# Keys, queries and values of a tile as one fp32 product in a two-layer GNN kernel

## Chip, core and metric

The kernel runs on one core of a Trainium2 chip. The metric is the device time of one execution in microseconds (us). Engines are named as in the profile: PE is TensorE (PEld its weight loads), ACT is ScalarE, DVE is VectorE, POOL is GpSimd, SP is the engine that issues most transfers. Everything discussed here happens in the first of two stages, in which node features and the tables for the second stage are made.

## What is computed

There are 6250 nodes of 128 features, 200000 edges sorted by destination, 4 node types and 8 edge types. The first layer averages the neighbours of each node, applies a linear layer and normalises. The second layer is an attention over edges; its queries, keys and values are products with a matrix that depends on the type of the node.

```python
def _type_matmul(h, W, types):
    out = jnp.zeros_like(h)
    for t in range(W.shape[0]):
        out = out + jnp.where((types == t)[:, None], h @ W[t], 0.0)
    return out

x = _layernorm(x + relu(concat([x, neigh_mean]) @ W.T + b))      # first layer
Q, K, V = (_type_matmul(x, W, node_type) for W in (W_Q, W_K, W_V))
k_t = _type_matmul(K[src], W_edge, edge_type)                    # per edge
scores = jnp.sum(Q[dst] * k_t, axis=-1) / scale * mu[edge_type]
out = segment_sum(V[src] * sparse_softmax(scores, dst)[:, None], dst)
x = _layernorm(x + out)
```

## The kernel before

**Two stages.** The nodes are cut into 49 tiles of 128. The first stage (up to about 1360 us of the profiled span) sums the neighbours, computes the first layer for each tile and writes, for each node, 8 rows (one for each edge type) of key times edge matrix beside the value, to the table `kv_table` in HBM, and the queries to `queries_t`. The second stage (the rest of the span) gathers table rows for each edge and does the attention. The change touches the first stage only.

**The sweep.** `sweep(l0)` goes through 50 steps `i`. On PE, step `i` is a loop over `h` = 0 to 48. Each `h` is one bf16 matmul of 385 columns (`slot_sum`, L715) for the neighbour sums; at every third `h` comes a `pick` (L708, 392 columns), whose result ACT copies (`take`, L1007) before the pick after next may be written to the same PSUM bank. Groups of 8 matmuls (`run_sum`, L738) stand at `h` = 0 and 22, and `node_sum` (L727) at `h` = 3 waits for DVE's `join_parts` (L1280). All engines work strictly in the order in which their instructions are written.

**What a tile needs inside the sweep.** In step `i` the tile `i - 2` ("early") gets its first layer: PE transposes (L745 at `h` = 30, L750 at 35) and the product L755 to L757 at 40, then DVE's `relu` (L1336) and `normalise_x1`, which leaves `x1_typed`: the tile's rows, one copy for each of the 4 types, zeroed where the node has another type. The tile `i - 3` ("late") gets its projections: at `h` = 8 PE transposes the four copies (L763) and ACT copies them to SBUF (L1024, after take 3). At `h` = 13 `project_keys` (L771) multiplies with `wk_s` as the stationary operand, so that the keys come out transposed, at `h` = 16 `project_values` (L776) with the rows as stationary operand, so that values come out as rows, and at `h` = 19 `project_queries` (L780), again transposed. Each is four fp32 matmuls of 128 columns added up in PSUM. ACT copies the transposed keys to `kT` after take 5 (`copy_key`, L1028) and, after take 7, the values 8 times over into `kv_rows` (L1034, which also waits until the previous tile's table rows are stored) and the queries to `q_tile` (L1037). Then PE multiplies the keys with the edge matrices, `low_keys` (L786, `h` = 25) and `high_keys` (L789, `h` = 28), 512 columns each; DVE copies the low half (L1357) and ACT the high half (L1041), and SP stores.

**Order.** Nothing schedules this by itself: the numbers `h ==` on PE and `c ==` on ACT are the order. 47 tiles have their late part inside the sweep (steps 3 to 49). Step 49 has no picks. The last two tiles have it behind the sweep in `late_part`, where the same functions follow one another with nothing between them.

**PSUM.** Keys go to bank 7, shared with `node_sum` and `high_keys`; values and queries to bank 5, shared with the first layer's transposes and product.

## Time and profile before

| | us |
|---|---|
| median of 3 runs | 3727.59 (3725.5 to 3731.58) |
| the profiled execution, whole | 3697.22 |
| its span, first to last instruction | 3695.4 |

The rows quoted below come from that one profiled execution. PE, ACT, DVE, POOL busy over the whole span: 2551.0, 1124.1, 1530.9 and 2372.2 us. An fp32 matmul shows as two records ("x8" for four matmuls); an fp32 transpose is one record. A record of PE is drawn longer than the time that it holds the engine, because matmuls are pipelined: the next one starts while the record before is still open. What a matmul costs is therefore read from start to start.

### The profile page before, as it was taken

The numbers are of one execution on the slowest core, as the hardware profiler recorded it, in microseconds if no ns is written. First come the engines' busy times: TensorE is split into PE (matmuls) and PEld (weight loads), VectorE is DVE, ScalarE is ACT, GpSimd is POOL, SyncE is SP. The second block draws the span as 40 slices with busy tenths as digits, with TensorE's granted clock in tenths as the row PEclk, the third lists the DMA queues.
The fourth block names the chain that finished last, engine by engine and source line by source line (L and its number), as shares of the span: only waits on it lengthen the run. The fifth ranks groups of instructions, "written<-read, shape, count | busy, mean of one in ns | idle before, by whom it ended". The sixth has DMA issues, their size and how long they took to land.

```text
span 3695.4 us, 38864 instructions
## 1 busy us (share of the span) xinstructions
PE 2551.0 (69%) x13692; PEld 1754.7 (47%) x13692; DVE 1530.9 (41%) x4283; ACT 1124.1 (30%) x2072; POOL 2372.2 (64%) x2400
## 2 busy tenths in 40 slices
PE   1688888888888861666666666666676666666667
PEld 0355555555555541444444444444444444444445
DVE  8466666666666620222222222222222222222223
ACT  3333444444444420222222222222222222222222
POOL 6656667676666617566666666666666666666662
PEclk9799999999999985777777777777777777777778
DMA  4233344443444313233333333333333333333331
GB/s 135 64 98 115 107 130 120 119 120 107 120 120 120 112 68 107 72 96 96 97 97 96 97 97 96 97 97 96 97 97 97 97 97 96 96 97 97 97 97 43
DMA packets 195810, 369.81 MB, mean 100 GB/s; under 512 B 62177, under 2 KB 126509, under 8 KB 189347
## 3 DMA queue, kind: packets, MB, share of 16 engines
q0 software_dynamic: 112432, 281.92, 27.5%
q1 hardware_dynamic: 76679, 82.09, 6.7%
q10 hardware_dynamic: 6508, 3.33, 0.3%
q8 instruction: 111, 1.82, 0.2%
q14 instruction: 80, 0.66, 0.1%
HBM read 299.89 MB, written 67.30 MB: 99 GB/s over the span
## 4 chain that ended last, share of the span: by engine, by line
PE 38%; another core or an unknown queue 20%; issue 19%; ACT 14%; DVE 8%; ACTq 1%; DMA 0%; DVEq 0%; POOLq 0%; POOL 0%; SPq 0%
PE banks L715 8%; ACT work L1090 5%; PE banks L872 4%; PE banks L886 4%; PE banks L901 3%; PE banks L708 3%; ACT work L1098 3%; ACT picks L1007 2%; PE banks L738 2%; DVE sums L1269 2%; PE banks L771 1%; PE banks L908 1%; PE banks L866 1%; PE banks L776 1%
## 5 line engine op out<-in xcount | busy, mean ns | idle before, releaser
L655 POOL DMA_INDIRECT ring<-kv_table,src_n x1264 | 1207.9, 956 | 625.9 <-issue 368.8
L650 POOL DMA_INDIRECT ring<-x_part_rows,work x512 | 538.0, 1051 | 249.2 <-issue 138.4
L886 PE MATMUL banks<-identf,ring 128*128 128x128 f32 x1264 | 242.9, 319 | 646.5 <-ACT work L1098 458.2
L1007 ACT ACTIVATE picks<-banks 128x392 bf16<-128x392 f32 x800 | 396.6, 499 | 730.0 <-PE banks L708 646.7
L715 PE MATMUL banks<-sums,picks 128*128 128x385 bf16 x2450 | 617.6, 335 | 0.4 <-ACT picks L1007 0.4
L886 PEld LDWEIGHTS banks<-identf,ring 128*128 128x128 f32 x1264 | 169.4, 162 | 698.9 <-ACT work L1098 506.4
L1090 ACT ACTIVATE work<-banks,negmax 128x2048 f32<-128x2048 f32 x98 | 193.0, 1969 | 905.9 <-issue 668.4
L1098 ACT ACTIVATE work<-banks 128x512 f32<-128x512 f32 x392 | 213.0, 598 | 816.1 <-remote 689.1
L1467 DVE SCALAR_TENSOR_TENSOR sums<-sums,corr,banks 128x128 f32<-128x128 f32 x98 | 34.0, 347 | 936.5 <-remote 928.9
L1448 DVE TENSOR_REDUCE largest<-banks 128x1 f32<-128x2048 f32 x98 | 224.6, 2292 | 468.9 <-PE banks L872 252.3
L872 PE MATMUL banks<-work,queries 128*128 128x512 f32 x784 | 412.2, 674 | 4.1 <-issue 4.1
L655 POOL DMA_INDIRECT sums<-kv_table,src_n x304 | 290.5, 956 | 143.5 <-issue 87.1
L650 POOL DMA_INDIRECT src_n<-x_part_rows,work x256 | 273.3, 1068 | 132.9 <-issue 71.2
L1500 DVE COPY sums<-banks 128x512 f32<-128x512 f32 x392 | 265.3, 690 | 213.4 <-PE banks L901 127.3
L901 PE MATMUL banks<-identf,work 128*128 128x128 f32 x1568 | 329.6, 398 | 31.8 <-issue 20.2
L901 PEld LDWEIGHTS banks<-identf,work 128*128 128x128 f32 x1568 | 315.4, 219 | 34.6 <-issue 21.0
L1268 DVE TENSOR_SCALAR sums<-iota_n,keys_g 128x128 bf16<-128x128 bf16 x800 | 216.8, 271 | 268.8 <-PE banks L708 249.7
L715 PEld LDWEIGHTS banks<-sums,picks 128*128 128x128 bf16 x2450 | 242.3, 101 | 179.5 <-issue 67.3
L908 PEld LDWEIGHTS banks<-ring,sums 128*128 128x128 f32 x2528 | 294.6, 192 | 40.7 <-issue 39.3
L908 PE MATMUL banks<-ring,sums 128*128 128x128 f32 x2528 | 295.1, 275 | 1.1 <-DVE sums L1500 1.1
L708 PE MATMUL banks<-sums 128*128 128x392 bf16 x800 | 270.2, 339 | 34.6 <-issue 23.2
L1269 DVE TENSOR_SCALAR sums<-iota_k,keys_g 128x392 bf16<-128x392 bf16 x800 | 274.6, 343 | 0.0
(279 smaller groups left out, 2785.7 us busy)
## 6 DMA issues: line engine op xcount, KB each, us to landing
kv_table<-ring SPq DMA_DIRECT2D x49, 1024.0 KB
ring<-kv_table,src_n POOLq DMA_INDIRECT x1264
ring<-x_part_rows,work POOLq DMA_INDIRECT x512
sums<-kv_table,src_n POOLq DMA_INDIRECT x304
x_part_rows<-sums SPq DMA_DIRECT2D x7, 675.5 KB, 4.5
src_n<-x_part_rows,work POOLq DMA_INDIRECT x256
sums<-x_rows SPq DMA_DIRECT2D x51, 64.0 KB, 1.9
x_rows<-ring SPq DMA_DIRECT2D x49, 64.0 KB
```

Of the source, the lines that this page charges most:

```text
L650: pool.indirect_dma_start(near[k % RUNS][:, j, :], None, part_dram, bass.IndirectOffsetOnAxis(ap=col_ids[:, first + j:first + j + 1], axis ...
L655: pool.indirect_dma_start(kv_ring[u][:, j, :], None, table, bass.IndirectOffsetOnAxis(ap=of, axis=0)).then_inc(l1_rows[2 * u + j // RUN], 16)
L708: pe.matmul(bank[c % 2][:, 0:KEYS], hot_low[:, c % HOT_RING, :], hot_key[:, c % HOT_RING, :], start=True, stop=True).then_inc(pick_ps, 1)
L715: mm = pe.matmul(bank[2 + i % 2][:, 0:3 * D + 1], picked[:, i % 2, h, :], x_parts[:, h, 0:3 * D + 1], start=(h == 0), stop=(h == TILES - 1))
L872: mm = pe.matmul(bank[g], queries[:, :], keysT[:, g, :], start=False, stop=True, skip_group_check=True)
L886: tr = pe.transpose(bank[KEY_BANK[g]][:, j * P:(j + 1) * P], kv_ring[k.u][:, g * 4 + j, 0:D], identf[:, :])
L901: tr = pe.transpose(bank[PROB_BANK[g]][:, j * P:(j + 1) * P], probT[:, at:at + P], identf[:, :])
L908: mm = pe.matmul(bank[7][:, 0:D], prob[:, j, :], kv_ring[k.u][:, j, D:2 * D], start=(j == 0), stop=(j == COLS - 1))
L1007: act.activation(picked[:, par, :, c * NW:(c + 1) * NW], bank[c % 2][:, 0:KEYS].rearrange("p (h w) -> p h w", w=NW), ACT.Copy).then_inc(pi ...
L1090: act.activation(probT, scores, ACT.Exp, bias=negmax[:, k.par:k.par + 1], accum_out=part_sum[:, k.par:k.par + 1]).then_inc(prob_ready, 1)
L1098: act.activation(keysT[:, g, :], bank[KEY_BANK[g]], ACT.Copy).then_inc(keysT_ready, 1)
L1269: ins = dve.tensor_scalar(hot_key[:, c % HOT_RING, :], iota_k[:, :], keys_g[:, par, 0, c:c + 1], None, ALU.is_equal)
```

## The change

The three products become one. The weights of the three matrices are laid side by side in SBUF for each type (`w_vkq`, 384 columns: values, keys, queries), and `project` at `h` = 13 uses the typed rows as the stationary operand and these 384 columns as the moving one: four fp32 matmuls of 384 columns into bank 5. Keys and queries now come out as rows and not transposed. After take 5 ACT copies both at once (256 columns) to a new tile `kq_rows` and, right behind it, the values into `kv_rows`. At `h` = 20 PE transposes the keys and the queries (`transpose_kq`, two fp32 transposes into bank 7), and after take 7 ACT copies them to `kT` and `q_tile`. The matmuls at `h` = 16 and 19 are gone. `high_keys` now waits until the queries have left bank 7.

```diff
-        wq_s, wk_s, wv_s = (by_type(ring_part(NT * D)) for _ in range(3))
+        w_vkq = ring_part(NT * 3 * D).rearrange("p (t c) -> p t c", c=3 * D)
+        wv_s, wk_s, wq_s = (w_vkq[:, :, k * D:(k + 1) * D] for k in range(3))
...
-            def project_keys(tile, sums):
+            def project(tile):
+                pe.wait_ge(typedT_ready, tile.t + 1)
+                for t in range(NT):
+                    mm = pe.matmul(bank[5][:, 0:3 * D], x1_typedT[:, t, :], w_vkq[:, t, :], start=(t == 0), stop=(t == NT - 1))
+                mm.then_inc(vkq_ps, 1)
+
+            def transpose_kq(tile, sums):
                 pe.wait_ge(acc_added, sums)
-                pe.wait_ge(typedT_ready, tile.t + 1)
                 pe.wait_ge(kw_high, tile.t + 1)
-                for t in range(NT):
-                    mm = pe.matmul(bank[7][:, 0:P], wk_s[:, t, :], x1_typedT[:, t, :], start=(t == 0), stop=(t == NT - 1))
-                mm.then_inc(k_ps, 1)
-
-            def project_values(tile):
-                for t in range(NT):
-                    pe.matmul(bank[5][:, 0:P], x1_typedT[:, t, :], wv_s[:, t, :], start=(t == 0), stop=(t == NT - 1))
-
-            def project_queries(tile):
-                for t in range(NT):
-                    mm = pe.matmul(bank[5][:, P:2 * P], wq_s[:, t, :], x1_typedT[:, t, :], start=(t == 0), stop=(t == NT - 1))
-                mm.then_inc(q_ps, 1)
+                pe.wait_ge(kq_copied, tile.t + 1)
+                for k in range(2):
+                    tr = pe.transpose(bank[7][:, k * P:(k + 1) * P], kq_rows[:, k * D:(k + 1) * D], identf[:, :])
+                tr.then_inc(kqT_ps, 1)
...
             def high_keys(tile):
+                pe.wait_ge(q_copied, tile.t + 2)
...
                         if h == 13:
-                            project_keys(late, added(i))
-                        if h == 16:
-                            project_values(late)
-                        if h == 19:
-                            project_queries(late)
+                            project(late)
+                        if h == 20:
+                            transpose_kq(late, added(i))
...
-            def copy_key(tile):
-                act.wait_ge(k_ps, tile.t + 1)
-                act.activation(kT, bank[7][:, 0:P], ACT.Copy).then_inc(kT_ready, 1)
-
-            def copy_projected(tile):
-                act.wait_ge(q_ps, tile.t + 1)
+            def copy_rows(tile):
+                act.wait_ge(vkq_ps, tile.t + 1)
+                act.activation(kq_rows[:, :], bank[5][:, D:3 * D], ACT.Copy).then_inc(kq_copied, 1)
                 if tile.t > 0:
                     act.wait_ge(row_stored, tile.t * 16)
-                act.activation(kv_rows[:, :, D:2 * D], bank[5][:, 0:P].unsqueeze(1).broadcast_to([P, ET, D]), ACT.Copy
+                act.activation(kv_rows[:, :, D:2 * D], bank[5][:, 0:D].unsqueeze(1).broadcast_to([P, ET, D]), ACT.Copy
                                ).then_inc(v_spread, 1)
+
+            def copy_kq(tile):
+                act.wait_ge(kqT_ps, tile.t + 1)
+                act.activation(kT, bank[7][:, 0:P], ACT.Copy).then_inc(kT_ready, 1)
                 act.wait_ge(q_stored[tile.k], (tile.turn + 1) * 16)
-                act.activation(q_tile[:, tile.k, :], bank[5][:, P:2 * P], ACT.Copy).then_inc(q_copied, 1)
+                act.activation(q_tile[:, tile.k, :], bank[7][:, P:2 * P], ACT.Copy).then_inc(q_copied, 1)
...
                     if late and c == 5:
-                        copy_key(late)
+                        copy_rows(late)
                     if late and c == 7:
-                        copy_projected(late)
+                        copy_kq(late)
```

In the order of PE, between `h` = 13 and 20 of one step, the rows before are these (L715 is `slot_sum`, L708 `pick`, L771, L776 and L780 the keys, values and queries):

```order
L771 MATMUL banks<-work,ring 128x128 [waits kw_high,typedT_ready,acc_added]
L771 MATMUL banks<-work,ring 128x128 x3
L715 MATMUL banks<-sums,picks 128x385 x2
L708 MATMUL banks<-sums 128x392 [waits picked_ready]
L715 MATMUL banks<-sums,picks 128x385
L776 MATMUL banks<-ring,work 128x128 x4
L715 MATMUL banks<-sums,picks 128x385 x2
L708 MATMUL banks<-sums 128x392 [waits picked_ready]
L715 MATMUL banks<-sums,picks 128x385
L780 MATMUL banks<-work,ring 128x128 x4
```

The same place on PE in the changed kernel (L718 is now `slot_sum`, L711 `pick`, L772 the one product, L780 the two transposes):

```order
L772 MATMUL banks<-ring,work 128x384 [waits typedT_ready]
L772 MATMUL banks<-ring,work 128x384 x3
L718 MATMUL banks<-sums,picks 128x385 x2
L711 MATMUL banks<-sums 128x392 [waits picked_ready]
L718 MATMUL banks<-sums,picks 128x385 x3
L711 MATMUL banks<-sums 128x392 [waits picked_ready]
L718 MATMUL banks<-sums,picks 128x385 x2
L780 MATMUL banks<-identf,kq_rows 128x128 [waits kq_copied,kw_high,acc_added]
L780 MATMUL banks<-identf,kq_rows 128x128
```

Twelve matmuls of 128 columns have become four of 384 and two transposes; the waits on bank 7's last readers moved to the transposes, and a wait on ACT's copy was added there.

On ACT, from takes 4 and 5 of the same step on, before (L1007 is `take`):

```order
L1007 ACTIVATE picks<-banks 128x49x8 [waits pick_ps] x2
L1028 ACTIVATE ring<-banks 128x128 [waits k_ps]
L1007 ACTIVATE picks<-banks 128x49x8 [waits pick_ps] x2
L1034 ACTIVATE ring<-banks 128x8x128 [waits row_stored,q_ps]
L1037 ACTIVATE q_tile<-banks 128x128 [waits q_stored1]
```

The same place on ACT in the changed kernel (L1005 is now `take`):

```order
L1005 ACTIVATE picks<-banks 128x49x8 [waits pick_ps] x2
L1026 ACTIVATE kq_rows<-banks 128x256 [waits vkq_ps]
L1029 ACTIVATE ring<-banks 128x8x128 [waits row_stored]
L1005 ACTIVATE picks<-banks 128x49x8 [waits pick_ps] x2
L1034 ACTIVATE ring<-banks 128x128 [waits kqT_ps]
L1036 ACTIVATE q_tile<-banks 128x128 [waits q_stored1]
```

The eightfold copy of the values moved from behind take 7 to behind take 5, ahead of takes 6 and 7; the copy to `kT` moved behind take 7.

## Rows read from the trace of the kernel before

**Rows 1.** The page: busy tenths of PE and its granted clock (40 slices).

```profile
PE   1688888888888861666666666666676666666667
...
PEclk9799999999999985777777777777777777777778
```

**Rows 2.** Waits of PE from 200 to 1380 us: who waited for whom, total, times, longest.

```profile
PE banks L727 <- DVE sums L1280: 102.3, 47, 4.1
PE banks L755 <- ACT ring L1016: 27.6, 47, 0.6
```

**Rows 3.** Waits of DVE in the same stretch.

```profile
DVE ring L1336 <- PE banks L757: 61.2, 47, 4.3
```

**Rows 4.** Timeline of PE, one step: start, drawn us, instruction [idle before].

```profile
912.54 1.13 PE L771 MATMUL banks<-work,ring 128*128 128x128 f32 x8 [0.30 <-issue]
913.51 0.49 PE L715 MATMUL banks<-sums,picks 128*128 128x385 bf16 x2
913.84 0.33 PE L708 MATMUL banks<-sums 128*128 128x392 bf16 x1
...
914.17 1.05 PE L776 MATMUL banks<-ring,work 128*128 128x128 f32 x8
915.06 0.49 PE L715 MATMUL banks<-sums,picks 128*128 128x385 bf16 x2
...
915.72 1.05 PE L780 MATMUL banks<-work,ring 128*128 128x128 f32 x8
...
919.24 1.02 PE L786 MATMUL banks<-ring 128*128 128x512 f32 x2
920.10 0.49 PE L715 MATMUL banks<-sums,picks 128*128 128x385 bf16 x2
```

**Rows 5.** Timeline of PE, same step: transposes without and with a wait.

```profile
922.11 0.27 PE L745 MATMUL banks<-identf,ring 128*128 128x128 f32 x1
922.22 0.65 PE L715 MATMUL banks<-sums,picks 128*128 128x385 bf16 x3
...
923.91 0.33 PE L750 MATMUL banks<-identf,ring 128*128 128x128 f32 x1 [0.54 <-ACT picks L1007]
924.07 0.33 PE L715 MATMUL banks<-sums,picks 128*128 128x385 bf16 x1
```

**Rows 6.** Timeline of ACT, same step.

```profile
914.20 0.50 ACT L1007 ACTIVATE picks<-banks 128x392 bf16<-128x392 f32 x1 [1.37 <-PE banks L708]
914.60 0.27 ACT L1028 ACTIVATE ring<-banks 128x128 f32<-128x128 f32 x1
...
917.95 1.02 ACT L1034 ACTIVATE ring<-banks 128x1024 f32<-128x1024 f32 x1
...
923.56 0.30 ACT L1012 ACTIVATE ring<-banks 128x128 f32<-128x128 f32 x1
```

**Rows 7.** Groups by line on ACT, 1364 to 1380 us: a copy of 256 columns.

```profile
L1106 ACT ACTIVATE sums<-banks 128x256 f32<-128x256 f32 x1 | 0.4, 384 | 0.0
```

**Rows 8.** Timelines of two other steps: pick 5 and its take.

```profile
215.65 0.33 PE L708 MATMUL banks<-sums 128*128 128x392 bf16 x1
216.80 0.50 ACT L1007 ACTIVATE picks<-banks 128x392 bf16<-128x392 f32 x1 [2.16 <-issue]
...
1010.27 0.33 PE L708 MATMUL banks<-sums 128*128 128x392 bf16 x1
1011.13 0.50 ACT L1007 ACTIVATE picks<-banks 128x392 bf16<-128x392 f32 x1 [1.86 <-PE banks L708]
```

**Rows 9.** Timeline of the last tile's late part, behind the sweep.

```profile
1356.60 1.02 PE L786 MATMUL banks<-ring 128*128 128x512 f32 x2
1356.80 1.03 ACT L1034 ACTIVATE ring<-banks 128x1024 f32<-128x1024 f32 x1 [2.32 <-PE banks L780]
...
1357.72 0.27 ACT L1037 ACTIVATE q_tile<-banks 128x128 f32<-128x128 f32 x1
```

**Rows 10.** A table store: its issue, and the stretch behind it.

```profile
923.38 0.32 SPq L496 DMA_DIRECT2D kv_table<-ring  x1
...
924.00:928.00 4.00, 3.41 (x20) 2.05 (x21) 2.71 (x12) 1.42 (x4) 3.09 (x4) 1.00 0.98 340
```

The last three numbers of the stretch are PE's granted clock, the DMA share and GB/s.

More of the change, by code:

```diff
@@ L135, in gnn_kernel @@
         more_belongs = sb("more_belongs", [P, RUN * P // 2])
+        kq_rows = sb("kq_rows", [P, 2 * D])
         run_sums = sb("run_sums", [P, D + 1])
@@ L305, in gnn_kernel @@
         typedT_ready = sem("typedT_ready")
-        k_ps = sem("k_ps")
-        q_ps = sem("q_ps")
+        vkq_ps = sem("vkq_ps")
+        kq_copied = sem("kq_copied")
+        kqT_ps = sem("kqT_ps")
         q_copied = sem("q_copied")
@@ L824, in late_part @@
                 transpose_typed(tile)
-                project_keys(tile, added(ND))
-                project_values(tile)
-                project_queries(tile)
+                project(tile)
+                transpose_kq(tile, added(ND))
                 low_keys(tile)
@@ L1065, in late_part @@
                 copy_typed(tile)
-                copy_key(tile)
-                copy_projected(tile)
+                copy_rows(tile)
+                copy_kq(tile)
                 copy_high(tile)
```

## The prediction

> **What bounds the kernel now.** First the page's slices: PE is busy 8 tenths in the first stage at a clock mostly of 9 tenths, and 6 tenths afterwards [rows 1]. The change lies in the first stage alone. The second stage's instructions stay as they are, so I carry its time over unchanged.
>
> Within the first stage I ask for the waits. PE waits for DVE at `node_sum` in every step (102.3 us in 47 waits, 2.2 us a step) [rows 2], and DVE waits for PE at `relu` in every step (61.2 us in 47 waits, 1.3 us a step) [rows 3]. Two engines that wait for each other once a step form one loop: `node_sum` on PE, then PE's work from `h` = 3 to the product at `h` = 40 (L757), then `relu`, `normalise_x1`, hot matrices and `join_parts` on DVE, then `node_sum` again. The 2.2 us in which PE stands are therefore no cushion for work that lies between `h` = 3 and 40: such work delays L757, hence `relu`, hence `join_parts`, hence the wait's end by the same amount. PE's other regular waits, for ACT's copies of the first layer's transposes (L1016 is the longer) [rows 2], start from PE's own pick 9 and its transpose, behind the place of the change, so they move with it and absorb nothing. The projections stand at `h` = 13 to 20, inside that stretch, and PE has no hole there: from 912.54 on each block starts where the one before stops streaming [rows 4]. So what PE's own sequence gains or loses there counts in full, once for each tile.
>
> **What the change removes on PE.** From start to start: the keys 913.51 - 912.54 = 0.97 us, the values 915.06 - 914.17 = 0.89, and the queries, drawn with the same 1.05 us as the values, 0.89 as well, together 2.75 us [rows 4]. Each block is 8 passes (four fp32 matmuls of two records), 0.89 / 8 = 0.11 us a pass.
>
> **What it adds on PE, the product.** 8 passes of 384 columns. The trace has no such pass, but one on either side: 128 columns at 0.11 us, and 512 columns at (920.10 - 919.24) / 2 = 0.43 us [rows 4]. 0.43 / 512 is 0.84 ns a column; a narrow pass at that price is 0.107 us, 8 of them 0.86, and the 0.89 measured leaves 0.03 for a block's entry (0.11 for the keys' block, whose wait for L1024's copy empties the pipe). So a column costs the same narrow or wide, the weight loads are already hidden, and 384 columns are 0.32 us. The product: 8 x 0.32 + 0.11 = 2.68 us. Against 2.75 the gain is 0.07 us, the two entries that are gone. The bubble of 0.30 us ahead of the block [rows 4] stays, since the wait for the typed copy stays at `h` = 13. The number of fp32 columns streamed is the same, 12 x 128 = 4 x 384.
>
> At this place the Trainium skill speaks for the change: "TensorE: Matmul & The Clock Gate", section "Back-to-back issue gap", gives about 81 ns for a load and matmul of 128 columns and 131 ns for 512. By a straight line between them 384 columns would be 1.4 narrow ones and not 3; the trace's fp32 passes do not show this (0.11 and 0.43 us). What the time would be by it is a rival below.
>
> **What it adds on PE, the transposes.** A transpose whose wait is met costs 922.22 - 922.11 = 0.11 us; one for which PE had to wait costs 924.07 - 923.91 = 0.16 us behind the wait, since its weights were not loaded ahead [rows 5]. Whether the new pair waits is a race that I work out from the start of pick 5. On ACT: take 5 starts 914.20 - 913.84 = 0.36 us after it, the next ACT instruction 0.40 later [rows 4, 6]; the copy of 256 columns takes 0.38 [rows 7]; so `kq_rows` is there at 0.36 + 0.40 + 0.38 = 1.14. PE resumes 0.05 us after an ACT copy (L1012 ends 923.86, L750 starts 923.91) [rows 5, 6], which makes 1.19. On PE: pick 5, slots 15 to 17, pick 6, slots 18 and 19 are seven streams of 0.165 (from 913.51 to 914.17 there are four, in 0.66) [rows 4], so PE arrives at 1.15. It waits 0.04 us and loses its load-ahead: 0.04 + 0.16 + 0.11 = 0.31, taken as 0.32 us. Lower bound 0.22 (two met transposes); upper bound below.
>
> **On ACT.** One copy more (0.38 us a tile), and the values' eightfold copy of 1.02 us [rows 6] stands ahead of takes 6 and 7. Behind it on ACT are queued take 6, take 7, the copies to `kT` and `q_tile`. I count from pick 5's start: `kq_rows` 1.14, values about 2.1, take 6 2.5, take 7 2.9, `kT` 3.3, `q_tile` 3.6. PE needs take 6 for pick 8 (`h` = 24): 1.47 + slot, pick, slot 0.5 + `run_sum` 1.3 + two slots 0.33 = 3.6. It needs `kT` at `h` = 25, about 0.4 later, 4.0, and the queries out of bank 7 at `h` = 28, 1.5 later still. All are met, by 0.7 us in the nearest case; cost nothing. The cover is `run_sum` between pick 7 and pick 8; without its 1.3 us PE would wait some 0.6 us for `kT`. The values' copy also waits until the previous tile's table rows are stored, and it now asks for that 1.3 us earlier. The store of 1 MB issued at 923.38 falls into a stretch of 4 us with 340 GB/s, 1.36 MB, ending at 928 [rows 10]; the next copy into the same rows comes a step after 917.95 [rows 6], near 942 (a step is (1010.27 - 913.84) / 4 = 24.1 us [rows 4, 8]): some 14 us to spare, cost nothing. SP's stores still wait for the high half, L1041.
>
> **A tile inside the sweep:** -0.07 + 0.32 = +0.25 us. 46 tiles have picks around them: 46 x 0.25 = 11.5 us. Tile 46 (step 49, no picks, ACT free) has met transposes: +0.15.
>
> **The last two tiles**, behind the sweep, have nothing between the functions. Before, `low_keys` started at 1356.60, right behind the queries [rows 9]. After, it waits: product's end to the start of an ACT copy 1356.80 - 1356.60 = 0.20, the copy of 256 columns 0.28 until the next begins (0.38 less the 0.10 by which ACT's records overlap), the values 1357.72 - 1356.80 = 0.92, `kT` 0.27, release 0.05: 1.72, less the 0.07: +1.65 us each [rows 7, 9]. This is ACT's order, not PE's work: the values' copy stands ahead of `kT`. Both lie on the chain to the end of the stage: 3.3 us.
>
> **Sum:** 11.5 + 0.15 + 3.3 = 15.0 us. The profiled execution took 3697.22 us, which would become 3712.2. The median of the runs is 3727.59, 30 us above the profiled one; I add the same 15.0 and forecast 3742.6.
>
> **Rivals.**
>
> *A: the wide product is cheaper a column (faster).* Place: the product at `h` = 13. It decides from the point where the product costs 2.75 - 0.32 - 3.3 / 47 = 2.36 us or less, a pass of 0.28 instead of 0.32. The far bound is a bf16 stream of 385 columns, 0.165 us [rows 4]: 8 x 0.165 + 0.11 = 1.43, so -1.32 + 0.32 = -1.00 a tile, -47 + 3.3 = -44 us, 3684. Against it stands the 512-column pass at 0.43 us in the same step, with the same kind of operands. The page's figures named above make 8 x 0.107 x 1.4 + 0.11 = 1.31 us as an estimate, and some 3679 us. Chance 0.04; 0.03 more for a gain that I cannot place, from the second stage's granted clock, which runs at 7 tenths [rows 1] and may fall otherwise when everything shifts.
>
> *B: the pair of transposes is hardly felt (no change).* If ACT's copy came before PE in the race and the transposes were met: 0.22 - 0.07 = +0.15 a tile, 7 + 3.3 = 10 us, 3738. That is still slower. To stay below 7.5 us it needs besides that the last two tiles cost nothing or that the runs' own scatter (6 us between lowest and highest of three) hides it. Chance of a result within the bound 0.17.
>
> *C: pick 5's signal is late (slower still).* In most steps take 5 starts 0.36 us after pick 5, but not in all: the first exception starts pick 5 at 215.65 and its take at 216.80, the last at 1010.27 and 1011.13 [rows 8]; there are 8 of them in 48 tiles, 0.2 to 1.5 us each and 7 us in all. Before, nobody waited for ACT at this place; now PE waits for the copy behind take 5. If all of them land on the transposes: 15 + 7 = 22 us, 3750. Chance 0.25, inside "slower".
>
> *D: ACT's longer queue stops PE at pick 8 or at `low_keys`.* It needs 0.7 us more on ACT than counted. Then 46 x some 0.5 us more: 38 us, 3766. Chance 0.05.
>
> *E: the change doesn't do what it says.* It does: the order of PE shows four matmuls of 384 columns and two transposes. No chance is set aside.
>
> **How the numbers follow.** The forecast (10 to 20 us) has 0.46, C 0.25, D 0.05, B 0.17, A and the clock 0.07. A difference of 0.2%, 7.5 us, is about what a measurement of this kernel can tell from no change. So faster 0.07, same 0.17, slower 0.76. Range: the low end takes most of B with the scatter, 3730; the high end takes C with the scatter of the runs, 3757. A and D are left out, 0.12, and some tail of the rest.
>
> **What would show it.** In the profile after: L772's eight passes start to start 2.6 to 2.7 us; L780 0.27 us and a wait of PE for ACT L1026 of 0.05 to 0.2 us (idle as drawn some 0.2 more) in nearly every step; steps 0.25 us longer than the 24.1 us of before; `node_sum`'s wait unchanged near 2 us; `low_keys` of the last two tiles 1.7 us later behind the product. It would be wrong if the steps kept their length although L772 takes 2.7 us (then the loop is not the bound), or if L772 took clearly less than 2.6 (rival A).

## The result and the profile after

| | us |
|---|---|
| before, median of 20 runs | 3725.14 (3715.33 to 3737.07) |
| after, median of 20 runs | 3734.26 (3725.21 to 3743.06) |
| after / before | 1.0027, 95% interval 1.0019 to 1.0034 |
| the profiled execution of after, whole, and its span | 3733.18, 3731.4 |

The change makes the kernel slower, by 9.1 us (7 to 13 by the interval). On two other chips the same pair lay 24 us (medians) and 23 us (single executions) apart; that difference is taken up below.

The two profiled executions lie 36 us apart, four times the medians' 9.1, because the one of before had fallen 28 us under its own median. By the start of the last `high_keys` (1357.46 and 1374.32, shown below) 16.9 us of the 36 lie in the first stage and 19.1 in the second, whose instructions the change leaves as they are. What the two traces are good for is the shape of a step, not the total.

The page of after, the lines of [rows 1]: PE's busy tenths and its granted clock keep their shape.

```profile
PE   1688888888888861666766666666666666666666
...
PEclk9799999999999985777777777777777777777778
```

The waits of PE from 200 to 1380 us in after (engine, line waited for: us in total, times, longest), against [rows 2], and under them DVE's wait of [rows 3]:

```profile
PE banks L730 <- DVE sums L1279: 96.9, 47, 4.0
PE banks L758 <- ACT ring L1014: 27.6, 47, 0.6
...
PE banks L786 <- ACT ring L1034: 1.3, 2, 0.7
PE banks L780 <- ACT kq_rows L1026: 1.1, 2, 0.6
```

```profile
DVE ring L1335 <- PE banks L760: 62.3, 48, 4.3
```

L730 is `node_sum` now, L760 the end of the first layer's product. The loop between PE and DVE stands as before. L780, the new pair of transposes, has a drawn wait in two steps only, and L786 (`low_keys`) too: those are the last two tiles. In the sweep ACT's longer queue never stops PE at pick 8 or at `low_keys`.

The timeline of PE in one step of after (start, drawn us, instruction), the stretch that answers to [rows 4]; the last row is the slot of `h` = 20, behind the transposes:

```profile
919.28 2.85 PE L772 MATMUL banks<-ring,work 128*128 128x384 f32 x8
921.97 0.49 PE L718 MATMUL banks<-sums,picks 128*128 128x385 bf16 x2
922.30 0.33 PE L711 MATMUL banks<-sums 128*128 128x392 bf16 x1
...
923.58 0.41 PE L780 MATMUL banks<-identf,kq_rows 128*128 128x128 f32 x2
923.83 0.33 PE L718 MATMUL banks<-sums,picks 128*128 128x385 bf16 x1
```

And ACT in the same step, against [rows 6]:

```profile
922.66 0.50 ACT L1005 ACTIVATE picks<-banks 128x392 bf16<-128x392 f32 x1 [3.04 <-PE banks L711]
923.06 0.38 ACT L1026 ACTIVATE kq_rows<-banks 128x256 f32<-128x256 f32 x1
923.32 1.03 ACT L1029 ACTIVATE ring<-banks 128x1024 f32<-128x1024 f32 x1
924.23 0.90 ACT L1005 ACTIVATE picks<-banks 128x392 bf16<-128x392 f32 x2
924.98 0.32 ACT L1034 ACTIVATE ring<-banks 128x128 f32<-128x128 f32 x1
925.14 0.33 ACT L1036 ACTIVATE q_tile<-banks 128x128 f32<-128x128 f32 x1
```

The product takes 921.97 - 919.28 = 2.69 us start to start. The transposes: the two slots at 923.12 have streamed by 923.12 + 2 x 0.165 = 923.45, the next slot starts at 923.83, so the pair costs 0.38 us; 0.13 of it lie ahead of its start, a wait too short to be drawn as one. The copy into `kq_rows` ends 923.44, as the race had it (1.14 after pick 5 at 922.30).

**A step in five pieces.** Each piece runs from one start to the next and is the median over steps 11 to 46 of the profiled execution; for the first, steps with the full clock only. In us:

| from `node_sum` to `low_keys` | to `relu` | to the typed rows | to `join_parts` | to the next `node_sum` | a step |
|---|---|---|---|---|---|
| before 10.28 | 7.90 | 2.69 | 2.33 | 0.98 | 24.19 |
| after 10.55 | 7.90 | 2.69 | 2.18 | 0.98 | 24.31 |

The five add up to the step: this is the loop of the prediction, and the change lengthens its first piece by 0.27 us, where 0.25 was forecast. The fourth piece, eight vector operations of DVE behind the typed rows, is 0.15 us shorter in this trace of after; more on it below.

**The last two tiles.** The timeline of PE behind the sweep of after, against [rows 9] (in brackets the idle time ahead and who ended it), and ACT's copies there:

```profile
1366.25 5.49 PE L772 MATMUL banks<-ring,work 128*128 128x384 f32 x8 [0.69 <-ACT work L1022]
1372.30 0.47 PE L780 MATMUL banks<-identf,kq_rows 128*128 128x128 f32 x2 [0.57 <-ACT kq_rows L1026]
1373.39 1.10 PE L786 MATMUL banks<-ring 128*128 128x512 f32 x2 [0.61 <-ACT ring L1034]
1374.32 1.02 PE L790 MATMUL banks<-ring 128*128 128x512 f32 x2
```

```profile
1371.78 0.38 ACT L1026 ACTIVATE kq_rows<-banks 128x256 f32<-128x256 f32 x1 [5.58 <-PE banks L772]
1372.06 1.02 ACT L1029 ACTIVATE ring<-banks 128x1024 f32<-128x1024 f32 x1
1372.96 0.28 ACT L1034 ACTIVATE ring<-banks 128x128 f32<-128x128 f32 x1
```

The same stretch before, for its first and last row:

```profile
1352.12 2.05 PE L771 MATMUL banks<-work,ring 128*128 128x128 f32 x8 [0.73 <-issue]
1353.95 1.91 PE L776 MATMUL banks<-ring,work 128*128 128x128 f32 x8
1355.66 1.10 PE L780 MATMUL banks<-work,ring 128*128 128x128 f32 x8
...
1357.46 1.02 PE L789 MATMUL banks<-ring 128*128 128x512 f32 x2
```

From the product to `high_keys` it is 1374.32 - 1366.25 = 8.07 us, and was 1357.46 - 1352.12 = 5.34: +2.7 us, and +2.8 for the tile ahead of it; 5.6 us together in this pair of traces. Tile 46, in step 49, took 6.24 us and 6.08 before: +0.16.

### The profile page after: what moved, and what is told of

Same layout as the page of the kernel before. It is cut to its first block, busy times and chain, and to the rows that moved or that the text cites. A ratio compares the mean times of both kernels' runs of the same rounds, so it can differ in the third digit from the quotient of the medians.

```text
span 3731.4 us, 37493 instructions
## 1 busy us (share of the span) xinstructions
PE 2616.3 (70%) x13006; PEld 1704.3 (46%) x13006; DVE 1524.6 (41%) x4283; ACT 1134.7 (30%) x2121; POOL 2364.6 (63%) x2400
## 4 chain that ended last, share of the span: by engine, by line
PE 42%; issue 19%; another core or an unknown queue 18%; ACT 11%; DVE 10%; DMA 0%; POOL 0%; DVEq 0%; POOLq 0%; SPq 0%; ACTq 0%
PE banks L718 7%; PE banks L870 5%; PE banks L884 5%; PE banks L899 4%; ACT work L1089 4%; PE banks L772 4%; PE banks L711 3%; PE banks L906 3%; ACT work L1097 2%; ACT picks L1005 2%; PE banks L741 2%; PE banks L864 2%; DVE sums L1268 1%; PE banks L786 1%
## 5 line engine op out<-in xcount | busy, mean ns | idle before, releaser
L884 PE MATMUL banks<-identf,ring 128*128 128x128 f32 x1264 | 299.5, 341 | 633.1 <-issue 399.8
L1005 ACT ACTIVATE picks<-banks 128x392 bf16<-128x392 f32 x800 | 396.3, 499 | 731.3 <-PE banks L711 559.1
L718 PE MATMUL banks<-sums,picks 128*128 128x385 bf16 x2450 | 611.9, 336 | 1.2 <-issue 1.2
L884 PEld LDWEIGHTS banks<-identf,ring 128*128 128x128 f32 x1264 | 183.6, 169 | 727.8 <-issue 458.2
L870 PE MATMUL banks<-work,queries 128*128 128x512 f32 x784 | 401.6, 659 | 5.0 <-issue 5.0
L718 PEld LDWEIGHTS banks<-sums,picks 128*128 128x128 bf16 x2450 | 242.7, 101 | 207.3 <-issue 81.7
L711 PE MATMUL banks<-sums 128*128 128x392 bf16 x800 | 271.2, 341 | 39.2 <-issue 21.8
```

The costliest lines, as they stand in the source:

```text
L711: pe.matmul(bank[c % 2][:, 0:KEYS], hot_low[:, c % HOT_RING, :], hot_key[:, c % HOT_RING, :], start=True, stop=True).then_inc(pick_ps, 1)
L718: mm = pe.matmul(bank[2 + i % 2][:, 0:3 * D + 1], picked[:, i % 2, h, :], x_parts[:, h, 0:3 * D + 1], start=(h == 0), stop=(h == TILES - 1))
L870: mm = pe.matmul(bank[g], queries[:, :], keysT[:, g, :], start=False, stop=True, skip_group_check=True)
L884: tr = pe.transpose(bank[KEY_BANK[g]][:, j * P:(j + 1) * P], kv_ring[k.u][:, g * 4 + j, 0:D], identf[:, :])
L1005: act.activation(picked[:, par, :, c * NW:(c + 1) * NW], bank[c % 2][:, 0:KEYS].rearrange("p (h w) -> p h w", w=NW), ACT.Copy).then_inc(pi ...
```

## The experiments

All times are medians; a ratio is against the kernel before in the same session on the same chip, since chips differ (before took 3349.01 us on one and 3701.7 on another; the second stage's granted clock was 0.84 on the first and 0.77 on the second). On the first of these chips, that of the four kernels from "product alone" to "behind the loop", there is no trace of the kernel before or of after: where their steps are compared with before's or after's, those are the steps of the traces from other chips, which agree with each other within 0.01 us in piece 1. "Half-clock steps" are steps 11 to 46 whose stretch from `node_sum` to `low_keys` is 0.3 us or more above the shortest, with the sum of what they lose; "early" is what the eight steps 3 to 10 lose above the same base. "Piece 1" is from `node_sum` to `low_keys` at the full clock.

| kernel | ratio, 95% | us more or less | piece 1 | step | half-clock steps (us) | early, us |
|---|---|---|---|---|---|---|
| before (first trace) | | | 10.28 | 24.19 | 5 (5.7) | 8.2 |
| after (first trace) | 1.0027, 1.0019 to 1.0034 | +9.1 | 10.55 | 24.31 | 5 (7.1) | 10.6 |
| product alone | 1.0028, 1.0016 to 1.0040 | +9.6 | 10.18 | 24.04 | 15 (20.8) | 7.5 |
| transposes later | 1.0031, 1.0018 to 1.0043 | +10.6 | 10.39 | 24.26 | 6 (6.9) | 8.2 |
| 512 columns | 1.0289, 1.0274 to 1.0305 | +96.0 | 11.40 | 25.27 | 26 (38.9) | 13.7 |
| behind the loop | 0.9726, 0.9711 to 0.9741 | -91.8 | 8.50 | 22.37 | 0, see text | 1.4 |
| before again | one execution | -3.2 | 10.28 | 24.19 | 5 (5.7) | 10.7 |
| after again | 1.0070, 1.0055 to 1.0084 | +23.8 | 10.55 | 24.43 | 10 (12.5) | 8.1 |
| before, wait filled | 0.9959, 0.9945 to 0.9974 | -13.7 | 10.29 | 24.20 | 0 | 1.6 |
| after, wait filled | 1.0006, 0.9997 to 1.0015 | +2.8 | 10.55 | 24.43 | 0 | 3.6 |
| before, one gather | one execution | -41.2 | 10.27 | 24.13 | 6 (7.3) | 7.9 |
| after, one gather | one execution | -17.1 | 10.54 | 24.39 | 9 (11.2) | 10.2 |
| after, third time | one execution | +22.7 | 10.55 | 24.43 | 10 (12.4) | 12.8 |

### Which of the two edits costs what

**The product alone.** The wide product stays; the two transposes go, and ACT copies keys and queries straight on, so that both are left untransposed and the output is not the reference's.

```diff
-                        if h == 20:
-                            transpose_kq(late, added(i))
...
-                act.activation(kq_rows[:, :], bank[5][:, D:3 * D], ACT.Copy).then_inc(kq_copied, 1)
+                act.activation(kT, bank[5][:, D:2 * D], ACT.Copy).then_inc(kT_ready, 1)
```

> This kernel has the one product of 384 columns, but no transposes: the keys and the queries are copied as the rows that they are, by ACT at the places of the kernel before (so keys and queries are not transposed and the output is not the reference's). My theory: the product alone is worth the two block entries, 0.06 us a step, 3 us over the sweep, and PE's stretch from node_sum to low_keys is 10.28 - 0.06 = 10.22 us in a quiet step, against 10.28 before and 10.55 after; the whole is 3715 to 3730 us beside a before of 3725. Rival one (the cost lies in the wide product or in its place, and the transposes are hidden): the stretch is 10.4 us or more without them. Rival two (the wide product is cheaper a column): the stretch is 10.0 us or less.

Measured: piece 1 falls from 10.28 to 10.18, so this edit saves 0.10 us a step. Only 0.06 of it is the products' own time, 2.69 instead of 2.75. The rest lies ahead of them: from the start of the slot before to the start of the product it is 0.58 us and was 0.62. The kernel is 9.6 us slower all the same, where 10 faster to 5 slower was expected. Its 46 steps give back 4.6 us, but 15 instead of 5 of them run partly at half clock, 15.1 us more. This was the first sign of a term that the prediction lacks.

**The transposes later.** The pair moves from `h` = 20 to `h` = 22, and its wait for ACT is met by then.

```diff
-                        if h == 20:
+                        if h == 22:
                             transpose_kq(late, added(i))
```

> The changed kernel with the two transposes at h = 22, ahead of run_sum, instead of h = 20: two slots and a pick (0.5 us) later, so that ACT's copy is there when PE arrives. My theory: PE loses the wait of 0.13 us and the lost load-ahead, and pays 0.22 to 0.25 us for the pair instead of 0.38 from stream end to next stream; node_sum to low_keys 10.42 us in a quiet step instead of 10.55, 6 us less than the changed kernel over the sweep, 1.001 times the kernel before. Rival (PE's wait for the copy is not what the pair costs): the stretch stays at 10.55 us.

Its timeline of PE in one step:

```profile
714.24 0.32 PE L718 MATMUL banks<-sums,picks 128*128 128x385 bf16 x1
714.40 0.38 PE L780 MATMUL banks<-identf,kq_rows 128*128 128x128 f32 x2
714.62 1.15 PE L741 MATMUL banks<-ring,more_belongs 128*128 128x385 bf16 x6
```

A met pair takes 714.62 - 714.40 = 0.22 us, the lower bound that the prediction gave. Piece 1 is 10.39: 0.21 above the product alone. With its short wait, in after, the pair costs 10.55 - 10.18 = 0.37. So the net 0.27 a step is -0.10 for the product, +0.21 for two met transposes and +0.16 for the wait and the slower start behind it.

The time of the whole did not follow: 10.6 us above before, where 3 were expected. Piece 1 explains 46 x 0.11 = 5.1 of it and the half-clock steps 1.2; the rest of the sweep behind step 46 and the last two tiles took 6 us more than in before's traces, 12 together. After itself was not run on this chip, so what the later place saves is seen in piece 1 and not in the time.

### Does PE's work between `h` = 3 and 40 count in full?

**512 columns.** The product's moving operand gets 128 columns more; what they give lands in a part of the bank that nobody reads.

```diff
-                    mm = pe.matmul(bank[5][:, 0:3 * D], x1_typedT[:, t, :], w_vkq[:, t, :], start=(t == 0), stop=(t == NT - 1))
+                    mm = pe.matmul(bank[5], x1_typedT[:, t, :], ring[:, t * 3 * D:t * 3 * D + 4 * D], start=(t == 0), stop=(t == NT - 1))
```

> The changed kernel with a product of 512 columns instead of 384; the 128 more go to a part of the bank that nobody reads. My theory: a column of a pass costs 0.84 ns at any width and PE's time there counts in full, so 8 x 0.107 = 0.86 us a step and 47 x 0.86 = 40 us more than the changed kernel, 1.0135 times the kernel before, and the pass in the trace is 0.43 us. Rival (a wide pass is cheaper a column, or PE's time there is partly cushioned by its wait at node_sum): less than 25 us more, with the wait at node_sum shorter than 1.83 us in a quiet step.

Measured: piece 1 is 11.40, 0.85 above after and the 8 x 0.107 us of 128 more columns: they count in full. A clean step is 25.27 us, 1.08 above before's: 50 us over 46 steps. Another 39 us are steps at half clock, 26 of them instead of 5 (33 us), and the early ones (5.5 us). That is 89 of the 96; what lies behind step 46 takes another 5. The whole is more than twice the 1.35% that was expected, and the excess is mostly the half-clock steps.

**Behind the loop.** The kernel before, with the values' and the queries' products taken out of the loop's stretch, to `h` = 46 and 48 (bank 6), where PE would otherwise soon stand still at `node_sum`; ACT's copies of them go to the end of its step. The wait for the queries' copy moves from the first layer's transposes to those of the typed rows, and ACT's copy of the high half gets a wait for the stored rows.

```diff
-                        if h == 16:
-                            project_values(late)
-                        if h == 19:
-                            project_queries(late)
+                        if h == 46:
+                            project_values(late, 6)
+                        if h == 48:
+                            project_queries(late, 6)
...
-                    if late and c == 7:
-                        copy_projected(late)
...
+                if late:
+                    copy_projected(late, 6)
```

> The kernel before, with the values' product moved from h = 16 to h = 46 and the queries' from h = 19 to h = 48, behind the first layer's product (h = 40) of the same step, and their copies on ACT to the step's end; nothing is left out. My theory: node_sum's wait for DVE is a cushion for what stands behind h = 40 and for nothing ahead of it. The 1.78 us leave the loop and fill PE's wait of 1.95 us, so a quiet step goes from 24.2 to some 22.4 us and the whole gets 75 to 85 us shorter, ratio 0.978. Rival one: POOL, which issues 16 gathers a step at 1.26 us and some 1.5 us of longer ones, becomes the bound near 22.5 to 23.5 us a step, ratio 0.982 to 0.992, with PE waiting for gathers at run_sum. Rival two (PE's total work is the bound, not the loop): no change, ratio 1.000.

Its wait at `node_sum`, 200 to 1230 us, and a step's start on PE:

```profile
PE banks L727 <- DVE sums L1286: 14.5, 25, 2.2
```

```profile
904.13 1.48 PE L738 MATMUL banks<-ring 128*128 128x385 bf16 x8
905.45 0.66 PE L715 MATMUL banks<-sums,picks 128*128 128x385 bf16 x3
905.95 0.33 PE L708 MATMUL banks<-sums 128*128 128x392 bf16 x1
906.42 0.71 PE L727 MATMUL banks<-sums 128*128 128x129 f32 x4
```

Piece 1 falls to 8.50, which is 10.28 less the two blocks' 2 x 0.89, and the step falls by the same 1.8 us; 102.3 us of standing at `node_sum` [rows 2] have become 14.5, with the same work done in that time. Over 46 steps that is 84 us, and 5.7 + 6.8 us come from half-clock steps that are no longer there. One step, that of 428.88, is 7.5 us longer than the others: PE waits for DVE at a pick (4.5 us drawn) and runs at half clock for a while behind it. Together 89 of the 92. The same products in another place: 2.7% faster than before, and the lowest ratio of all kernels here.

### Steps at half clock

**After again**, unchanged, beside the kernel before on another chip, shows the thing itself.

> The changed kernel, unchanged. Theory one: 0.27 us a clean step more than before (12.5 us over 46), 5.5 us for the last two tiles, plus or minus what half-clock stretches take, 1.2 to 1.7 us for each step that has one; ratio 1.003 to 1.007. Theory two (the DVE stretch from the typed rows to join is shorter by 0.14 us because of the change): the stretch is 2.18 us here too, a clean step only 0.13 us longer, ratio 1.003. If it is 2.31 us, as in the three kernels built from the changed one and the kernel before on this chip, the 0.14 us are not the change's.

> The kernel before, unchanged, for a profile on the chip of these experiments. Theory one (half-clock stretches decide): a clean step has node_sum to low_keys 10.28 us and join's start 2.31 us behind the typed rows; the granted clock falls to half behind PE's wait at node_sum in 0 to 6 of the 36 steps from 11 to 46. Theory two (the DVE stretch of 2.18 us in the changed kernel belongs to the change): nothing said of this run.

Two steps of it on PE, from `node_sum` (its wait in brackets) to the product. The first:

```profile
942.62 0.71 PE L730 MATMUL banks<-sums 128*128 128x129 f32 x4 [1.95 <-DVE sums L1279]
...
944.75 0.33 PE L711 MATMUL banks<-sums 128*128 128x392 bf16 x1
944.92 0.66 PE L718 MATMUL banks<-sums,picks 128*128 128x385 bf16 x3
...
946.16 2.85 PE L772 MATMUL banks<-ring,work 128*128 128x384 f32 x8 [0.25 <-ACT work L1022]
```

The next step:

```profile
967.05 0.71 PE L730 MATMUL banks<-sums 128*128 128x129 f32 x4 [1.94 <-DVE sums L1279]
...
969.99 0.53 PE L711 MATMUL banks<-sums 128*128 128x392 bf16 x1
970.31 1.17 PE L718 MATMUL banks<-sums,picks 128*128 128x385 bf16 x3
...
971.84 2.74 PE L772 MATMUL banks<-ring,work 128*128 128x384 f32 x8
```

Slices of the same trace (busy time of PE, PEld, DVE, ACT and POOL, then PE's granted clock, the DMA share and GB/s):

```profile
944.00:946.00 2.00, 1.91 (x13) 1.14 (x11) 1.86 (x11) 1.38 (x4) 1.48 (x2) 1.00 0.19 49
...
968.00:970.00 2.00, 2.00 (x11) 1.39 (x10) 1.48 (x7) 0.50 (x1) 1.70 (x2) 0.58 0.21 49
970.00:972.00 2.00, 2.00 (x8) 1.14 (x7) 1.44 (x7) 1.14 (x3) 1.39 (x3) 0.56 0.23 60
```

From `node_sum` to the product it is 3.54 us in one step and 4.79 in the next. After the same wait of 1.94 to 1.95 us the granted clock is 1.00 in the first and 0.58 and 0.56 in the second, and 0.50, the lower of the two levels (1.2 GHz), in the slices of 1 us from 969 to 971; a stream of 0.165 us takes 0.32. It comes back inside the step. The Trainium skill, "TensorE: Matmul & The Clock Gate", section "HAM oscillation", describes how a kernel that stops at a wait in each round can pay for the slow clock in each round. The traces here agree, with 1.1 to 1.7 us a time, but not in each round: 5 to 26 of 36.

The steps that lose it don't come at random. In before again they are steps 14, 22, 30, 38 and 46, each 8 behind the last; in the later transposes they lie 6 apart (once 7), in after again 2 to 5, and in the product alone, from step 18 on, they are pairs that return every 4 steps. Traces of a kernel with the same length of a step had the same count: 5 and 5 for before at 24.19 us, 10 and 10 for after at 24.43; in the first trace of after, where a step took 24.31, it was 5. This looks like a beat between the step and something with a period of its own. No run tests it, but if it is so, an edit can change the count merely by changing the step's length.

**The wait filled.** Ten bf16 matmuls into a bank that `node_sum` then overwrites stand ahead of its wait, in the kernel before and in after alike; their result is used by nobody.

```diff
-                pe.wait_ge(slots_vec, i * 3 + 9)
                 pe.wait_ge(acc_added, added(i) if i > 0 else 1)
...
+                for o in range(10):
+                    pe.matmul(bank[7][:, 0:3 * D + 1], iota_n[:, :], x_parts[:, o, 0:3 * D + 1], start=True, stop=True)
+                pe.wait_ge(slots_vec, i * 3 + 9)
```

> The kernel before with ten more bf16 matmuls of 385 columns (1.65 us) at h = 3, ahead of node_sum's wait for DVE, into a part of bank 7 that node_sum overwrites. Theory: PE waits 1.95 us there, so the ten cost nothing in a clean step; the short rest of the wait no longer lets the clock fall, so the steps at half clock (extra 1.2 to 2.3 us each, about 14 us in the sweep of the profiled execution) are gone, ratio 0.996 to 0.999. Rival (PE's time is the bound, or the wait is only drawn): 47 x 1.65 = 78 us more, ratio 1.023.

> The changed kernel with the same ten matmuls at the same place. Theory: no step at half clock inside the sweep either, so against the same filling of the kernel before only the plain terms are left: 46 x 0.27 + 0.1 + 5.5 for the last two tiles = 18 us, a ratio between the two filled kernels of 1.0054. Rival (the cost of the change is mostly half-clock steps and hardly the transposes): the two filled kernels lie within 5 us.

The kernel before with the filling, on PE:

```profile
946.52 1.81 PE L726 MATMUL banks<-sums,iota_n 128*128 128x385 bf16 x10
948.62 0.71 PE L729 MATMUL banks<-sums 128*128 128x129 f32 x4 [0.29 <-DVE sums L1282]
```

The idle time at `node_sum` shrinks to 0.29 us, the step keeps its length (24.20 against 24.19) and no step of 36 has a half-clock stretch in either kernel. Before gains 13.7 us; its half-clock steps, early ones included, had cost 16.4 us in the trace of before again and cost 1.6 here, 14.8 less. That the clock costs this much, and that it hangs on this wait, is shown by doing nothing but fill the wait. With both kernels filled, the change costs 3704.54 - 3688.02 = 16.5 us. Their steps differ by 24.43 - 24.20 = 0.23 us, 10.6 over 46, the early steps by 2.0, and the last two tiles take 4.2 us more: 16.8. (The first stages of the two traces lie 20.4 us apart, 3.1 of it ahead of step 3, which the change doesn't touch.)

The first of these two tiles runs at the full clock in both kernels (1.00 in the slices from its first product to `high_keys`). Before, filled:

```profile
1327.88 1.13 PE L773 MATMUL banks<-work,ring 128*128 128x128 f32 x8 [0.73 <-DVE ring L1294]
...
1331.49 1.02 PE L791 MATMUL banks<-ring 128*128 128x512 f32 x2
```

After, filled:

```profile
1344.12 2.85 PE L774 MATMUL banks<-ring,work 128*128 128x384 f32 x8 [0.69 <-ACT work L1024]
...
1349.56 1.02 PE L792 MATMUL banks<-ring 128*128 128x512 f32 x2
```

From product to `high_keys` it is 3.61 and 5.44 us: at the full clock the change costs such a tile 1.8 us.

### DVE's shorter stretch

Between the typed rows and `join_parts` the first trace of after had 2.18 us and before 2.33. One step of each kind, DVE's first of the eight operations and the copy behind the last, in after:

```profile
911.70 0.25 DVE L1267 TENSOR_SCALAR sums<-iota_n,keys_g 128x128 bf16<-128x128 bf16 x1
...
913.29 0.28 DVE L1276 COPY sums<-banks 128x129 f32<-128x129 f32 x1
```

and in after again:

```profile
939.92 0.25 DVE L1267 TENSOR_SCALAR sums<-iota_n,keys_g 128x128 bf16<-128x128 bf16 x1
...
941.64 0.28 DVE L1276 COPY sums<-banks 128x129 f32<-128x129 f32 x1
```

1.59 us against 1.72 for the same operations of the same kernel. Over 46 steps 0.15 us is 6.9 us. One theory was that POOL's gathers disturb DVE, and disturb it less when PE's work lies otherwise. So both kernels ran with one gather of a run's eight, whose rows stand in for the others (so the sums over neighbours are others than the reference's).

```diff
-                for j in range(RUN):
+                for j in range(1):
```

> The kernel before with one gather for each run of eight columns in the sweep instead of eight, and the run's eight matmuls reading that one column (so the neighbour sums are not the reference's): POOL is nearly silent in the sweep. Theory: in the DVE stretch from the typed rows to join's start (eight comparisons of 0.31 to 0.44 us and others) the longer comparisons come from POOL's gathers that fall on them; without gathers the stretch is 2.18 us or less in every clean step. Rival: the stretch depends on DVE alone and stays at 2.31 to 2.34 us.

> The changed kernel with the same cut in gathers (neighbour sums not the reference's). Theory: the DVE stretch is as short as in the kernel before without gathers, so that the two differ by 0.27 us in a clean step, node_sum to low_keys 10.28 and 10.55 us; if the stretches differ between the two, the change itself acts on DVE.

> The changed kernel once more, one look on another occasion: its DVE stretch from the typed rows to join was 2.18 us in the first profile and 2.33 us in the second. Theory (it belongs to the execution or the chip, by where POOL's gathers fall): either value, with the same value for all clean steps of this execution. Rival (it belongs to the kernel): 2.18 us.

Measured: with POOL almost silent (80 us busy in 1100 instead of 743) the stretch is 2.35 us in both, and it is 2.33 in after's third execution. The theory falls. The 2.18 belongs to one execution or to that chip, not to the change; what makes it is open. The steps hardly change by the missing gathers (24.13 against 24.19 and 24.39 against 24.43), and 35 of the 41 us by which before with one gather is shorter than before lie ahead of step 3. So the gathers do not bound the sweep. The pair lies 24.1 us apart: 46 x 0.26 = 12.0, the half-clock steps 6.2 and the last two tiles 5.5 (measured in this pair too) make 23.7.

## Why the prediction was right, and where it was not

The forecast was 3742.6 us, 15.0 above before; the median came to 3734.26, 9.1 above, inside the range, and slower as forecast.

- **What bounds the kernel.** Right. The loop `node_sum` to `low_keys` to `relu` to `join_parts` adds up to the step in every trace. Work added inside it counts in full (512 columns, +0.85 of 0.86), work moved out of it is gained in full (behind the loop, -1.8 of 1.78).
- **The product.** 2.68 was forecast, 2.69 measured; the saving -0.07 against -0.10, because the bubble ahead of the product, which was to stay, shrank from 0.30 to 0.25 us. A column costs the same in a narrow and in a wide fp32 pass. Rival A falls: neither 0.28 us a pass nor the figures of the section "Back-to-back issue gap" of "TensorE: Matmul & The Clock Gate" in the Trainium skill show here.
- **The transposes.** 0.32 forecast, 0.37 measured; met, 0.21 to 0.22 as bounded. The race with ACT's copy was read rightly from both timelines. Its sign was not: no wait is drawn at L780 in the sweep, where one was foretold in nearly every step, and the pair is drawn with 0.41 us and not 0.27. The net 0.25 us a step came out as 0.27. This is why rival B falls: the wait is met only at a later place, two slots and a pick on.
- **ACT's queue.** Right: no wait at pick 8 or `low_keys` in the sweep; rival D falls. **Late signals of pick 5** (rival C) did not land on the transposes: one drawn wait of L780 is in each of the last two tiles and none in the sweep. The late signals themselves are gone: from 200 us on take 5 starts 0.36 to 0.37 us after pick 5 in every step of after, and the same in after again, while before had 7 late ones there. That rival had 0.25, too much, and what delays them in before stays open.
- **The last two tiles.** This term was mis-sized: 3.3 us was forecast, and it measured 5.6, 5.5, 4.2 and 2.3 in the four pairs of traces (the first, one gather, filled, again). It counted ACT's order rightly: 1.65 us a tile, against 1.8 at the full clock. What it lacks is the clock. At this place PE often comes out of a wait at half clock. In the first pair, before, the third product of the last tile already ran mostly at full clock (0.94 us); the single wide one runs all 8 passes at half clock, 5.49 us drawn, and ACT can't begin until it ends.
- **What the sum lacked.** "`node_sum`'s wait unchanged near 2 us" was right, and the prediction took that for harmless. In some steps the clock falls behind that wait, and how many steps do so differs between kernels: 5 for before in two traces, 5, 10 and 10 for after, 15 for the product alone, 26 for 512 columns. For this change it is a term of +4 to +9 us by the traces and of 7.3 by the difference between the pair unfilled (23.8) and filled (16.5); for the product alone it is +15. The clock "mostly of 9 tenths" in [rows 1] doesn't show it, since a 9 is 90% or more and the filled kernels have the same 9s there; slices of 2 us do.
- **The size.** On the chip of the pair "again" the pieces add up in the traces: 46 x 0.24 = 11.0 for the steps, 4.2 for the half-clock steps up to step 46, 1.5 for one more behind it and 2.3 for the last two tiles make 19.0, and the first stages lie 18.9 us apart. The second stages differ by 2.0, and the medians by 23.8. On the first chip the steps give 46 x 0.12 = 5.5 (12.4 less 6.9 for DVE's shorter stretch), the last two tiles 5.6 and the half-clock steps 3.8: 14.9, against 16.9 between the traces' first stages. But the medians there are only 9.1 apart, so 5.8 us have no place. The second stage, which the prediction carried over unchanged, could hold them: it was 19.1 us longer in the first trace of after than in that of before, and within 4 us of the same in the other traces on one chip. How it behaved in the other runs of the first chip, and whether DVE's stretch was short in them, can't be seen, so the difference between the chips, 15 us, is not settled. The forecast's 15.0 lies between the 9.1 and the 23.8. The way was forecast by the right mechanism; that the number fell inside the range is in part luck: it lacked one term of 4 to 9 us, had another too small, and on the first chip DVE's shorter stretch and something that no trace explains took more than that off again.

## What to carry to other kernels

Where two engines wait for each other once a step, the step is the sum of the loop's pieces: an instruction on one side of the wait costs all of its time, and on the other nothing as long as the wait lasts. So ask first where it stands and only then what it is. Here the same two products, moved from inside the loop into the wait, gave 92 us, some 12 of them by the clock, twenty times the 0.10 us a step that merging saved. And a short wait of TensorE that comes back every step is not only idle time: look at the granted clock in slices of a few us behind it, since the number of steps that lose it varied here from edit to edit and blurred the results of small ones.

## What the runs showed of the hardware

- An fp32 matmul's pass cost 0.11 us for 128 columns, 0.32 for 384 (2.69 less the entry of 0.11, by 8) and 0.43 for 512: by the column. Merging three products of 128 columns into one of 384 saved 0.06 us of 2.75, and 0.05 us of a bubble ahead of it.
- Behind a wait of about 1.95 us TensorE's granted clock was sometimes 1.00 and sometimes 0.50 for the next microseconds, at 1.1 to 1.7 us a time. With the wait cut to 0.3 us by filling, this happened in none of 36 steps. The steps that fell came at even distances, and executions with the same length of a step had the same count; why one step falls and its neighbour doesn't, and why a step longer by 1 us raised the count from 5 to 26, stays open.
- A wait of PE for ACT that was too short to be drawn as idle (0.13 us) made a pair of transposes 0.38 us instead of 0.22.
- The same kernel differed by 0.15 us a step in DVE's stretch between two executions, with nothing in the kernel that explains it.
